# Hybrid scan and expert kernel: S5 constants set up behind the first sequence's steps, rotation in the first turn, W3 scaled on ScalarE

## What is computed

```python
x = x + s6(layernorm(x))      # selective scan: 256 channels x 64 states over 512 tokens
x = x + ffn(layernorm(x))     # 8 experts of 128 -> 256 -> 128, the best two weighted
x = x + s5(layernorm(x))      # diagonal complex scan, 64 states
x = x + ffn(layernorm(x))     # the same experts again
```

## Time and profile before

| | |
|---|---|
| median of three runs | 2012.18 us (2009.53 to 2018.62) |
| the profiled execution | 2013.24 us |
| its span in the trace | 2011.4 us |
| VectorE busy | 84% |
| GpSimd busy | 76% |
| TensorE (matmul) busy | 69% |
| ScalarE busy | 57% |

### The profile page before, as it was taken

One profiled execution on the slowest core, in us unless ns is written; L12 is line 12 of the kernel. 1 busy time (PEld: TensorE's weight loads), 2 busy tenths in 40 slices (PEclk: granted clock), 3 DMA queues, 4 the chain that ended last, 5 costly groups with the idle time before them and its releaser, 6 DMA issues. The chain is left out here.

```text
span 2011.4 us, 23542 instructions
## 1 busy us (share of the span) xinstructions
PE 1380.4 (69%) x5800; PEld 596.3 (30%) x5800; DVE 1688.7 (84%) x2401; ACT 1137.6 (57%) x2176; POOL 1521.2 (76%) x888
## 2 busy tenths in 40 slices
PE   3135358768776778768776778767786778668857
PEld 1001023224231333224332333323332333224424
DVE  5688989899898889898899889898898989896433
ACT  3456656665666556665557556655566565544313
POOL 0698998788987798787987798777997799874112
PEclk8557569889897989888887989878898889879869
DMA  1600400021001300031000400021000310000000
GB/s 51 235 0 24 170 8 1 24 105 68 12 1 55 142 11 0 24 105 69 11 0 28 169 11 0 24 105 69 11 0 24 136 43 0 1 6 1 6 0 6
DMA packets 34153, 88.25 MB, mean 44 GB/s; under 512 B 5363, under 2 KB 20598, under 8 KB 25846
## 3 DMA queue, kind: packets, MB, share of 16 engines
q1 hardware_dynamic: 32454, 87.12, 12.2%
q10 hardware_dynamic: 1584, 0.01, 0.0%
HBM read 75.58 MB, written 11.53 MB: 43 GB/s over the span
## 5 line engine op out<-in xcount | busy, mean ns | idle before, releaser
L855 POOL TENSOR_TENSOR w<-ur,br 128x1024 f32<-128x1024 f32 x512 | 1200.3, 2360 | 221.2 <-DVE h L1159 206.7
L1159 DVE TENSOR_TENSOR_SCAN h<-da,w 128x512 f32<-128x512 f32 x1024 | 1205.8, 1208 | 98.0 <-ACT da L746 38.8
L746 ACT ACTIVATE da<-dr,al 128x511 f32<-128x511 f32 x1024 | 691.2, 692 | 229.0 <-DVE h L1159 215.5
L575 PE MATMUL ys<-h,wsum 128*32 128x512 f32 x2048 | 333.4, 729 | 215.0 <-DVE h L1159 186.0
L513 PE MATMUL bankH<-nT,w 128*128 128x512 f32 x512 | 308.6, 687 | 111.8 <-DVE sq L1089 111.7
L694 ACT ACTIVATE tq<-bankH 128x512 f32<-128x512 f32 x256 | 153.0, 598 | 373.9 <-PE bankH L513 373.9
L513 PE MATMUL bankG<-nT,w 128*128 128x512 f32 x512 | 292.2, 654 | 63.0 <-DVE aq L1098 62.6
L526 PEld LDWEIGHTS bankY<-w,aq 128*128 128x128 f32 x2048 | 266.6, 205 | 115.4 <-issue 63.8
L526 PE MATMUL bankY<-w,aq 128*128 128x128 f32 x2048 | 272.6, 290 | 28.0 <-DVE aq L1098 19.7
L799 POOL TENSOR_TENSOR x<-x,yk 128x512 f32<-128x512 f32 x128 | 162.7, 1271 | 170.7 <-ACT yk L707 170.1
L1089 DVE SCALAR_TENSOR_TENSOR sq<-tq,bankH 128x512 f32<-128x512 f32 x256 | 170.6, 666 | 97.7 <-ACT tq L694 97.5
(11 more groups left out here) (175 smaller groups left out, 854.7 us busy)
## 6 DMA issues: line engine op xcount, KB each, us to landing
br<-b_rows SPq DMA_DIRECT2D x32, 1024.0 KB, 11.2
dr<-d_rows SPq DMA_DIRECT2D x16, 1024.0 KB, 7.1
ur<-u_rows SPq DMA_DIRECT2D x16, 1024.0 KB, 6.8
d_rows<-vh SPq DMA_DIRECT2D x16, 256.0 KB
u_rows<-th SPq DMA_DIRECT2D x16, 256.0 KB
xnew<-in_L_attn_a_x_dram SPq DMA_DIRECT2D x8, 256.0 KB, 3.2
w<-in_L_ffn_W_dram SPq DMA_DIRECT2D x2, 1024.0 KB, 14.6
x<-in_L_attn_a_x_dram SPq DMA_DIRECT2D x8, 256.0 KB, 7.7
```

The source lines that it names most:

```text
L575: ins = nc.tensor.matmul(ys[32 * q:32 * q + 32, :], wsum[:, :], h[:, (2 * group + q // 2) % H_RING, q % 2, :], start=(n == 0), stop=(n == ...
L746: A(da[duo % D_RING][:, k % 2, 1:L], dr[:, half, q, 1:L], ACT.Exp, scale=nega[:, QUADS * half + q, n:n + 1]).then_inc(decay_ready, 1)
L855: G.tensor_tensor(w[:, duo % W_RING, :, :], ur[:, half, q:q + 2, :], br[:, n:n + 1, :].to_broadcast([128, 2, L]), ALU.mult).then_inc(produ ...
L1159: V.tensor_tensor_scan(h[:, duo % H_RING, k % 2, :], da[duo % D_RING][:, k % 2, :], w[:, duo % W_RING, k % 2, :], 0.0, ALU.mult, ALU.add). ...
```

## The change

`diagonal_setup` begins at slot 100 in place of 78 (SETUP_AT), behind the steps at 98 and 99; the transposes go to slot 112 (MATRICES_AT), and ScalarE's exponential and sines to 98. The rotation becomes a task of its own, `rotation`, woven into VectorE's turn 0: the two memsets at slot 4, the nine wide blocks at slots 10, 16, ... 58, the nine angle doublings three slots behind each (13 to 61), and the last table `rT` at 61. W3 is scaled by ScalarE in turn 0, one expert at a time, at slots 52, 55, ... 73; TensorE's wait counts eight.

```diff
--- before.py
+++ after.py
@@ -65,9 +65,10 @@
 S5_AT = output_slot(1, E - 1) + SUM_LAG - 3
 GATES_AT, RES_AT = 24, 36
 PRE_AT = 68
-SETUP_AT = PRE_AT + 10
+SETUP_AT = PRE_AT + 32
 SETUP_ROWS_AT = PRE_AT + 9
-MATRICES_AT = PRE_AT + 40
+MATRICES_AT = PRE_AT + 44
+ROTATION_AT, ROTATION_STEP = 4, 6
 SCALE_AT = 52
 LN_AT = [PRE_AT - 6, 7, 16, S5_AT, MOE_AT[2] - 8]
 RSTD_LAG, NORM_LAG = 6, 6
@@ -520,7 +521,7 @@
                         else:
                             pe.wait_ge(drained["G"], t.before(f"g{m}_{2 * n + 1}") + 1)
                         if n == 0:
-                            pe.wait_ge(outputs_scaled, QUADS)
+                            pe.wait_ge(outputs_scaled, E)
                         for a in range(TT):
                             for k in range(2):
                                 ins = nc.tensor.matmul(p[:, a * 128:(a + 1) * 128], aq[:, (2 * n + k) % 4, a * 128:(a + 1) * 128],
@@ -623,7 +624,7 @@
                 yield PRE_AT + 1
                 act.wait_ge(late_loads, 16 * LATE_LOADS)
                 A(s5w[:, 0:1], s5p[:, 2:3], ACT.Exp).then_inc(diagonal_a, 1)
-                yield PRE_AT + 4
+                yield SETUP_AT - 2
                 act.wait_ge(angles_ready, 1)
                 A(s5w[:, 3:4], s5w[:, 2:3], ACT.Exp).then_inc(diagonal_a, 1)
                 A(s5w[:, 6:7], s5w[:, 4:5], ACT.Sin).then_inc(diagonal_a, 1)
@@ -724,6 +725,15 @@
             def late(t):
                 yield from moe(t, 2, True)
 
+            def scale_outputs():
+
+                for n in range(E):
+                    yield SCALE_AT + 3 * n
+                    if n == 0:
+                        act.wait_ge(expert_loads, 16 * EXPERT_LOADS)
+                    part = w3[:, n, :, :].rearrange("p k c -> p (k c)")
+                    A(part, part, ACT.Copy, scale=0.25).then_inc(outputs_scaled, 1)
+
             def skips(t):
 
                 b = t.b
@@ -746,7 +756,7 @@
                     A(da[duo % D_RING][:, k % 2, 1:L], dr[:, half, q, 1:L], ACT.Exp,
                       scale=nega[:, QUADS * half + q, n:n + 1]).then_inc(decay_ready, 1)
 
-                weave(pair, [skips(t)] + tasks_of(t, pre_a, post, late))
+                weave(pair, [skips(t)] + ([scale_outputs()] if known(t.b, 1) else []) + tasks_of(t, pre_a, post, late))
 
             turns(act, pre_a, scan, post, late, [setup(), diagonal_setup()])
 
@@ -765,15 +775,6 @@
                 G.tensor_tensor(nm[:, k, :], bag[:, k, :, 0], rs[:, k, :], ALU.mult).then_inc(rstd_ready[k], 1)
                 pool.wait_ge(rstd_ready[k], 4 * i + 3)
                 G.tensor_tensor(nm[:, k, :], nm[:, k, :], minus[:, :], ALU.mult).then_inc(rstd_ready[k], 1)
-
-            def scale_outputs():
-
-                for n in range(QUADS):
-                    yield SCALE_AT + 3 * n
-                    if n == 0:
-                        pool.wait_ge(expert_loads, 16 * EXPERT_LOADS)
-                    part = w3[:, 2 * n:2 * n + 2, :, :].rearrange("p e k c -> p (e k c)")
-                    G.tensor_scalar(part, part, 0.25, None, ALU.mult).then_inc(outputs_scaled, 1)
 
             def pre_a(t):
                 i = t.b + 1
@@ -855,7 +856,7 @@
                     G.tensor_tensor(w[:, duo % W_RING, :, :], ur[:, half, q:q + 2, :],
                                             br[:, n:n + 1, :].to_broadcast([128, 2, L]), ALU.mult).then_inc(product_ready, 1)
 
-                weave(pair, [gates(t)] + ([scale_outputs()] if known(t.b, 1) else []) + tasks_of(t, pre_a, post, late))
+                weave(pair, [gates(t)] + tasks_of(t, pre_a, post, late))
 
             turns(pool, pre_a, scan, post, late)
 
@@ -963,18 +964,27 @@
                 chain(V.tensor_copy(cc[:, 1, 0, :], cc[:, 0, 1, :]))
                 chain(V.tensor_scalar(cc[:, 1, 1, :], sct[:, :, 0], -1.0, None, ALU.mult))
                 v.sem_inc(matrices_ready, 1)
-                yield SETUP_AT + 11
-
+                yield MATRICES_AT + 2
+                v.wait_ge(matrices_turned, 1)
+                chain(V.tensor_copy(mb[:, :, :].rearrange("p n c -> p (n c)"), banks["Y"][:, 0:256]))
+                chain(V.tensor_copy(mc[:, :, :].rearrange("p n c -> p (n c)"), banks["Y"][:, 256:512]))
+                v.sem_inc(drained["Y"], 1)
+
+            def rotation():
+
+                S = lambda n: s5w[:, n:n + 1]
+                c_, s_, er = S(11), S(12), S(3)
+                yield ROTATION_AT
                 chain(V.memset(cosT[:, 0:1], 1.0))
                 chain(V.memset(sinT[:, 0:1], 0.0))
                 n = 1
                 while n < L:
-                    yield SETUP_AT + 10 + n.bit_length()
+                    yield ROTATION_AT + ROTATION_STEP * n.bit_length()
                     chain(V.tensor_scalar(rT[:, 0:n], sinT[:, 0:n], s_, None, ALU.mult))
                     chain(V.scalar_tensor_tensor(cosT[:, n:2 * n], cosT[:, 0:n], c_, rT[:, 0:n], ALU.mult, ALU.subtract))
                     chain(V.tensor_scalar(rT[:, 0:n], cosT[:, 0:n], s_, None, ALU.mult))
                     chain(V.scalar_tensor_tensor(sinT[:, n:2 * n], sinT[:, 0:n], c_, rT[:, 0:n], ALU.mult, ALU.add))
-                    yield SETUP_AT + 10 + n.bit_length()
+                    yield ROTATION_AT + ROTATION_STEP * n.bit_length() + 3
 
                     chain(V.tensor_tensor(S(19), s_, s_, ALU.mult))
                     chain(V.tensor_tensor(S(20), c_, s_, ALU.mult))
@@ -983,11 +993,6 @@
                     chain(V.tensor_scalar(s_, S(20), 2.0, None, ALU.mult))
                     n *= 2
                 chain(V.tensor_scalar(rT[:, :], cosT[:, :], 0.0, er, ALU.mult, ALU.add))
-                yield MATRICES_AT + 2
-                v.wait_ge(matrices_turned, 1)
-                chain(V.tensor_copy(mb[:, :, :].rearrange("p n c -> p (n c)"), banks["Y"][:, 0:256]))
-                chain(V.tensor_copy(mc[:, :, :].rearrange("p n c -> p (n c)"), banks["Y"][:, 256:512]))
-                v.sem_inc(drained["Y"], 1)
 
             def moments(k, i, at, src):
 
@@ -1159,7 +1164,7 @@
                     V.tensor_tensor_scan(h[:, duo % H_RING, k % 2, :], da[duo % D_RING][:, k % 2, :], w[:, duo % W_RING, k % 2, :],
                                          0.0, ALU.mult, ALU.add).then_inc(scanned, 1)
 
-                weave(pair, [take_sums(t.b, 0, t, HALF + SUM_AT - 1)]
+                weave(pair, [take_sums(t.b, 0, t, HALF + SUM_AT - 1)] + ([rotation()] if known(t.b, 1) else [])
                       + tasks_of(t, pre_a, post, late))
 
             turns(v, pre_a, scan, post, late, [setup(), diagonal_setup()])
```

## The result

The changed kernel takes **2037.04 us**, the median of four runs (2031.51 to 2038.59), where the kernel before took 2010.86 in the same sitting (2005.68 to 2018.62, four runs). The ratio is 1.0125 with a 95% interval of 1.0098 to 1.0151: slower, by 1.0 to 1.5%. The profiled execution took 2035.92 us with a span of 2033.7, which is 22.3 more than the span before.

What follows compares the result with a forecast made beforehand. It took paired VectorE scans and GpSimd products as the bounding chain, costing only turn 0: -18.9 + 6.4 + 32.4 - 2.5 + 0.4 = +17.8 us on 2013.24, giving 2031 us, range 1996 to 2043.

Steps and rivals of the forecast that it cites:

- start, to the first scan: Up to the first scan: steps start 16.25 us sooner, tanh 2.7 us sooner without table loads ahead; -18.9 us.
- first 62 slots, own work: First half of turn 0: VectorE's scans plus the rotation at unhindered durations take 89.9 us, +6.4 us.
- first 62 slots, waits for GpSimd: First half of turn 0: rotation instructions wait for GpSimd's products in flight, +3.6 us nine times; +32.4 us.
- second half, with the scaling: Rest of turn 0: -2.5 us from GpSimd's lateness taken back, +0.4 us for ScalarE's scalings.
- the named better bound: Start: -20 us if TensorE, idle 3.39 us ahead of its projections, is at its faster pace sooner.
- the third rival: Before the first scan: delayed constants hold it up, start gains 12 instead of 18.9 us, 2038 us; chance 0.03.
- The period of six slots: First half of turn 0: one wide block and one angle doubling with waits take 12.3 us, 8.7 by durations alone.
- The second rival: Rotation in turn 0: only a block's first instruction waits, a chain begun isn't broken into; 2009.9 us, chance 0.17.
- The first rival: Rotation in turn 0: VectorE's rotation and GpSimd's products run side by side, no waits; 1998.6 us, chance 0.27.
- the gates: Slots 27 to 36 of turn 0: GpSimd's gates of 1.2 us may add waits, some 3 us, outside the sum.
- "Nothing behind it.": Everything after turn 0: each turn begins with an empty product ring, so the first turn's shift carries through; nothing costed.
- the sign that would prove it wrong: Turns behind the first: the forecast is wrong altogether if they differ from those of before.

Runs made afterwards that it cites:

- experiment 1: Changed kernel with the rotation's scratch in PSUM (bank Y) and three one-column products as tensor_scalar; 1997.3 us, ratio 0.9947 to the kernel before.
- experiments 9 and 10: 9: kernel before with only W3's scaling moved to ScalarE, 2003.97 us. 10: changed kernel, rotation scratch in PSUM, W3 scaled by GpSimd again, 1997.56 us.
- 37 fills: Changed kernel without the rotation (constant tables), with 37 chained idle fills on VectorE ahead of the first steps; 1995.93 us, ratio 0.9939.
- experiment 6: Changed kernel with no rotation at all, its tables filled with constants, so S5 is not the reference's; 1996.68 us, ratio 0.9942.
- experiment 2: Kernel before with single VectorE instructions of several operand kinds, each two times, set between scans of the first turn; 2011.67 us in one run.
- experiment 11: Changed kernel with only ScalarE's exponential and sines back ahead of the first tanh (slot 72); 2046.84 us in one run.

## Why the prediction was right

The span grew by 22.3 us. It is made up of the same stretches as the forecast's sum:

| term | forecast | measured |
|---|---|---|
| start, to the first scan | -18.9 | -19.5 |
| first 62 slots, own work | +6.4 | +6.4 (126.3 - 36.3 - 83.6) |
| first 62 slots, waits for GpSimd | +32.4 | +36.3 (53.55 - 17.21) |
| second half, with the scaling | -2.1 | -0.9 |
| sum | +17.8 | +22.3 |

**The start.** Right step by step. The 16.25 us of constants and rotation and the 2.7 us of table loads carried through; the further 0.6 are TensorE's projections, which came after 0.48 us of idle time in place of 3.39 and took 1.43 in place of 2.07. That was the named better bound. The constants kept 6 us to spare, so the third rival fell.

**The waits.** The period of six slots was forecast at 12.3 us and is 12.3 (141.47 to 153.81), with the pattern foretold: 1.19 in the wide block's first instruction (L983's 1.44 less 0.25), next to nothing in the doubling's first, and a whole product in its second. The second rival, that a chain once begun isn't broken into, fell on exactly that row: L990 lies 0.04 us behind L989, and the next product still got in ahead of it. The first rival, side by side, fell with it; experiment 1 is the kernel in which it would have been true, and there its sum of -14.6 us for turn 0 meets -11.3 at the start of turn 1 and -16.0 in the span.

**The term that was mis-sized.** The 62nd scan was over 126.3 us after the first began, not 122. The 4 us lie in the waits, and they are the gates, which the forecast named at 3 us and left out. GpSimd's timeline has them at 93.23, 98.68, 102.20 and 115.29, each 1.26 long, and a rotation instruction waits for each, beside the products: 0.96 + 1.03 + 1.02 + 1.03 = 4.0 us. Three of the four:

```profile
93.33 1.18 DVE L984 SCALAR_TENSOR_TENSOR cosT<-cosT,s5w,rT 128x4 f32<-128x4 f32 x1
...
98.77 1.19 DVE L990 TENSOR_TENSOR s5w<-s5w 128x1 f32<-128x1 f32 x1
99.99 2.26 DVE L991 TENSOR_TENSOR s5w<-s5w 128x1 f32<-128x1 f32 x1
102.29 1.18 DVE L992 TENSOR_TENSOR s5w<-s5w 128x1 f32<-128x1 f32 x1
```

Without them 32.3 us of waits are left, where 32.4 were worked out. That this agrees to a tenth is in part luck: the first wide block waited 2.4 us in place of 1.19, since two of its instructions met a product, while the second instruction of each doubling waited 2.1 in place of 2.31. The own work was right: 126.3 less 36.3 of waits is 90.0, and 89.9 were worked out. Experiment 1, without any wait, needs 91.8 because its forms of the rotation take 1.9 longer.

**The second half** gave back 0.9 where 2.1 net were taken. The link was right (ScalarE waits 2.44 us for the statistics where it waited 3.30 in the earlier trace rows), but less of it reached the end of the turn. ScalarE's scalings took 0.40 us each, in the bounds of 0.37 to 0.71, and experiments 9 and 10 show what the forecast's sum held without saying so: the move frees GpSimd of work that alone is worth 5 us, and beside the rotation nothing.

**"Nothing behind it."** This step was right by the number, with luck, and too simple as a rule. From the start of turn 1 to the end the span has 1767.7 us before and 1767.6 after. But the single turns are not alike, which the forecast had named as the sign that would prove it wrong: turn 3 takes 233.07 us in place of 228.27 and turn 6 takes 227.32 in place of 230.67, turns 2, 4 and 5 differ by 1.0 to 1.3, and all of it cancels. Over the other kernels that rest goes from 1759.3 (37 fills) over 1763.0 (experiment 1) to 1775.9 (no rotation). So in these executions, one of each kernel, a change at the front carries through to within some 8 us either way, and the forecast didn't hold that much in its range. Part of that may be the spread of a kernel with itself: the four runs of the kernel before lie 13 us apart. Of the 24.8 us by which experiment 6 brought turn 1 forward, 16.6 were left in the span.

## What to carry to other kernels

Before small VectorE instructions are spread between scans that GpSimd feeds, look at what their operands are: with both inputs in SBUF even one column can wait for a whole GpSimd instruction (2.1 us), with one source in SBUF and the result there too, two columns wait as 256 do, and that wait stands in the duration, not in the idle time. Put one operand or the result in PSUM, or put the work where GpSimd has nothing to do; the first made the rotation's own instructions 1.9 us longer here and turned +1.25% into -0.5%. And a gain at the front of a long loop is measured at the end of the span, not at the start of the next turn.

## What the runs showed that I had not expected

- A one-source instruction of a single column doesn't wait beside a product (0.13, 0.19 and 0.21 us), one of two columns waits the whole of what is left, or for the next product (1.42 and 2.37).
- Delaying the same work by some 6 us made the kernel 7.9 us faster, and by 13.7 us cost nothing: turns 3 to 6 of all these kernels take 227 to 233 us, those of 232 and more with matmuls of 172 to 173 us and a granted clock of 0.86 or 0.87, those up to 229 with 165 to 171 (in experiment 2 once 172) and 0.87 to 0.90. The two groups touch at 0.87, so the clock alone doesn't tell them apart. A front-end gain can be given back turns later.
- TensorE's first projections have a pace that changes with a few us of delay: four matmuls of the same shape in 1.98 or in 3.71 us, at a granted clock that reads 1.00 in both stretches (20 to 26 us of the kernel after, 26 to 32 of experiment 11). No cause is shown.
